# A third row tile in the last steps of attention, five steps a tile, eight sets of row statistics

## The reference

```python
def attn(x):                       # Wq, Wk, Wv, Wo, bo
    q, k, v = heads(x @ Wq), heads(x @ Wk), heads(x @ Wv)
    scores = q @ k.T - slopes * abs(pos_k - pos_q)
    scores = where(pos_k > pos_q, -inf, scores)
    return (softmax(scores / 8) @ v) @ Wo + bo
def ffn(x):                        # w1, b1, w2, b2
    h = round_2^-8(x @ w1 + b1)
    h = round_2^-8(piecewise_linear_gelu(h))       # 33 break points
    return round_2^-8(h @ w2 + b2)
x = x + layernorm(attn(layernorm(x)))
x = x + layernorm(ffn(layernorm(x)))
```

## Time and profile before

| | |
|---|---|
| time, median of 3 runs | 1228.38 us (1227.55 to 1300.74) |
| profiled execution | 1228.59 us |
| span of its slowest core | 1227.1 us (the eight cores: 1222.7 to 1227.1) |
| busy, share of the span | PE 93%, ACT 80%, DVE 61%, POOL 15% |
| 640 to 678 us, of 38 us | ACT busy 38.00, PE 32.80, DVE 18.61 |
| 678 to 711 us, of 33 us | PE busy 29.25, DVE 19.95, ACT 16.86 |

### The profile page before, as it was taken

One profiled execution on the slowest core, in us unless ns is written; L12 is line 12 of the kernel. 1 busy time (PEld: TensorE's weight loads), 2 busy tenths in 40 slices (PEclk: granted clock), 3 DMA queues, 4 the chain that ended last, 5 costly groups with the idle time before them and its releaser, 6 DMA issues.

```text
span 1227.1 us, 26972 instructions; the slowest of 8 cores (1222.7 to 1227.1 us)
## 1 busy us (share of the span) xinstructions
PE 1139.3 (93%) x11162; PEld 640.9 (52%) x11298; DVE 751.6 (61%) x1613; ACT 983.1 (80%) x1217; POOL 180.9 (15%) x357
## 2 busy tenths in 40 slices
PE   2889989999999999999998899879999999999996
PEld 2565556666565666666564444434444444444443
DVE  7876533333434324343344589996888888888843
ACT  3449999999999999999999578887777777777720
POOL 4530010010100100000002243430111111111110
PEclk9999999999999999999999999989999999999999
DMA  9952532343433412111119965656333333333211
GB/s 260 268 158 59 96 72 52 70 83 66 84 57 61 79 34 44 38 23 32 28 36 198 219 219 155 161 118 150 112 112 112 112 112 121 120 122 111 77 69 69
DMA packets 62870, 128.00 MB, mean 104 GB/s; under 512 B 9238, under 2 KB 26134, under 8 KB 62108
## 3 DMA queue, kind: packets, MB, share of 16 engines
q1 hardware_dynamic: 53900, 101.10, 28.2%
q0 software_dynamic: 8848, 25.17, 13.6%
HBM read 117.84 MB, written 25.17 MB: 117 GB/s over the span
## 4 chain that ended last, share of the span: by engine, by line
PE 73%; DVE 13%; ACT 8%; DMA 3%; issue 2%; POOL 1%; SPq 0%; DVEq 0%; POOLq 0%; ACTq 0%
PE pW L948 18%; PE pF L875 14%; PE pjb L316 11%; PE S L409 9%; PE acc L462 9%; PE pjb L348 8%; ACT P L425 6%; DMA xst<-x_full 2%; PE pja L316 1%; DVE x L578 1%; DVE bst L235 1%; DVE bst L236 1%; DVE g L919 1%; DVE kst L326 1%; DVE g L913 1%
## 5 line engine op out<-in xcount | busy, mean ns | idle before, releaser
L425 ACT ACTIVATE P<-S,biasT 128x1024 bf16<-128x1024 f32 (+1 forms) x576 | 563.4, 1078 | 20.9 <-PE S L409 19.1
L875 PE MATMUL pF<-xl2T,w1s 128*128 128x512 bf16 x1002 | 257.7, 384 | 12.3 <-ACT cu L890 11.0
L948 PE MATMUL pW<-w2s,hq 128*128 128x512 bf16 x1003 | 250.8, 380 | 3.3 <-ACT pW L973 2.2
L462 PEld LDWEIGHTS acc<-V,P 128*128 128x128 bf16 x4352 | 162.6, 97 | 53.5 <-DVE ctx L480 11.3
L462 PE MATMUL acc<-V,P 128*128 128x66 bf16 x4352 | 179.1, 193 | 4.1 <-DVE ctx L480 2.4
L409 PE MATMUL S<-Q,K 64*128 64x512 bf16 (+3 forms) x1280 | 173.4, 349 | 8.4 <-ACT P L425 6.6
L875 PEld LDWEIGHTS pF<-xl2T,w1s 128*128 128x128 bf16 x1024 | 100.2, 99 | 132.1 <-ACT cu L890 12.8
L948 PEld LDWEIGHTS pW<-w2s,hq 128*128 128x128 bf16 x1024 | 100.3, 98 | 123.9 <-issue 3.9
L316 PE MATMUL pjb<-xlT,W 128*128 128x512 bf16 x572 | 152.3, 381 | 13.0 <-issue 6.5
L326 DVE CAST kst<-pjb 128x512 bf16<-128x512 f32 x81 | 56.0, 691 | 132.5 <-PE pjb L316 128.7
L890 ACT ACTIVATE cu<-pF,b1s 128x512 int32<-128x512 f32 x128 | 87.7, 685 | 59.2 <-PE pF L875 59.2
(11 more groups left out here) (91 smaller groups left out, 1064.9 us busy)
## 6 DMA issues: line engine op xcount, KB each, us to landing
w1s<-w1bf SPq DMA_DIRECT2D x128, 256.0 KB, 2.7
xst<-x_full SPq DMA_DIRECT2D x32, 512.0 KB, 9.8
K<-kst SPq DMA_DIRECT2D x128, 64.0 KB, 2.0
Q<-kst SPq DMA_DIRECT2D x128, 64.0 KB, 2.3
w1bf<-w POOLq DMA_DIRECT2D x32, 256.0 KB, 4.0
x<-x_full SPq DMA_DIRECT2D x16, 512.0 KB, 5.2
w2s<-w POOLq DMA_DIRECT2D x8, 1024.0 KB, 26.9
x2scr<-x SPq DMA_DIRECT2D x16, 512.0 KB, 4.2
```

Source lines behind the costliest of these rows:

```text
L425: t = put("scalar", lambda io: io.activation(out=P3[:, :, c0:512], in_=S[s][:].rearrange("p (o c) -> p o c", o=2)[:, :, c0:512], func=AF.E ...
L462: io.matmul(acc[:, q * 66:(q + 1) * 66], P[p][:, at:at + 128], zv[:, o, j, hh, :], start=st, stop=sp, skip_group_check=True),
L875: t = put("tensor", lambda io, c=c: io.matmul(pF[b][:], w1s[n % 4][:, c * 128:(c + 1) * 128], xl2T3[g][:, c, :], start=(c == 0), stop=(c = ...
L948: t = put("tensor", lambda io, ft=ft, hf=hf: io.matmul(pO[b][:, hf * 512:(hf + 1) * 512], slot_of(g, ft, tl), w2s[:, ft * 1024 + hf * 512: ...
```

## The change

Three row tiles instead of two go through `c_early` (EARLY = 3). One yield in each half of the projection and the one after the transposes are taken out, so that each copy out of PSUM is listed right behind the matmuls that it waits for, in the same visit: five steps a tile instead of eight, with `c_x2` still in the call after. `ctxTe` and `sume` stay two buffers each and are used in turn. The ring of row statistics has eight slots instead of four. The normalisation of tile 0 and the load for tile 4 come just after `c0(3)`, since `c_parts` starts at n = 3.

```diff
-    NS = 4
+    NS = 8
...
-        EARLY = 2
+        EARLY = 3
...
             C[j, "left"] = t
-            yield
-            t = put("vector", lambda io: io.tensor_copy(out=ctxTe[j][:], in_=pjT[:]),
+            t = put("vector", lambda io: io.tensor_copy(out=ctxTe[j % 2][:], in_=pjT[:]),
                     after=[t, proj_end], inc=True)
             pjs["free"][0] = C[j, "ct"] = t
             yield
...
-                        pj_b[:], ctxTe[j][:, c * 128:(c + 1) * 128],
+                        pj_b[:], ctxTe[j % 2][:, c * 128:(c + 1) * 128],
...
                 t = put("tensor", lambda io, sl=sl: io.matmul(
                     pj_b[:], ones[:], borow[:, sl], start=False, stop=True), after=[t_brow], inc=True)
-                yield
                 pjs["free"][0] = C[j, "a"] = put("vector", lambda io, sl=sl: io.tensor_copy(
-                    out=sume[j][:, sl], in_=pj_b[:]), after=[t, proj_end], inc=True)
+                    out=sume[j % 2][:, sl], in_=pj_b[:]), after=[t, proj_end], inc=True)
                 if hf == 1:
-                    C[j, "sum"] = sume[j]
+                    C[j, "sum"] = sume[j % 2]
                     c_sta(j)
                 yield
             c_x2(j)
...
         c0(EARLY)
+        for j in range(EARLY - 2):
+            c_xl(j)
+            c_load(j + 4)
 
         for n in range(EARLY, 7):
             for _ in c_parts(n):
```

## The result

The changed kernel takes 1236.96 us, median of 3 runs (1236.96 to 1237.2), against 1228.38 before. The ratio is 1.0072 with a 95% interval of 1.0058 to 1.0086: slower by 0.7%, inside the 2% that were counted as no change, but clear of the scatter. One of the three runs of the kernel before took 1300.74 us, with the cores of one die at a lower clock, and the ratio leaves it out. The span of the slowest core is 1235.4 us, 8.3 more than before.

A forecast was written before the change was run, and what follows sets the result against it. Chain taken to run through ACT's exponentials while early tiles are worked on, then DVE's x2 steps; 7.4 + 2.8 - 5.6 + 0 = +4.6 us gives 1233.0 us, forecast range 1229.5 to 1237.5, 8 in 10 from 1226 to 1238.5.

The forecast's parts named there:

- The period taken out of the serial stretch: Between attention's end and `f_mm(0)`: one tile fewer saves one period of DVE's x2 chain, 5.58 us.
- PE has room for the third tile: In attention: a tile's five visits cost PE 9.99 us against ACT's 10.2, so it barely fits; otherwise 0 to 1 us.
- The two waits: At both tile changes in attention: PE waits 4.1 us for `ctxTe`, ACT loses 3.2 and 4.2 us, 7.4 together.
- The low clock: Behind both waits PE drops to half clock, 1.5 us lost each time; 2.8 us taken, bounds 0 to 3.0.
- The transfer: Serial stretch: the x load for tile 4 lands about when x2 wants it; 0 us, up to 2 as bound.
- rival (b): Waits covered or small, but tile 4's x load holds x2 in the serial stretch: 1228 us, -1.5 to +2; chance 0.19.
- From `f_mm(0)` on one to one: From the first feed-forward matmul to the end: same order of work, so the +4.6 us shift carries through unchanged.
- Rival (a): Waits in attention covered, third tile free, serial stretch gives back its period: 1223.3 us without the transfer; chance 0.13.

The follow-up runs named there:

- x2 in two parts: Changed kernel with an early tile's `c_x2` cut in two, x2 itself and its statistics listed in separate visits; ratio 1.0015 to the kernel before.
- The w1 loads behind the x loads: Kernel with x2 in two parts, with SP's four w1 loads listed behind the x loads of tiles 4 and 5; 1223.97 us, ratio 0.9970.
- the statistics behind: The 1223.97 us kernel with an early tile's row statistics also listed behind the next tile's copy to `ctxTe`; 1223.9 us, ratio 0.9969.
- x2 behind the copy: Changed kernel with a tile's `c_x2` listed behind the next tile's copy to `ctxTe` instead of ahead of it; ratio 1.0022 to the kernel before.
- the first experiment: Kernel before with five steps a tile and still two early tiles; ratio 1.0064 to the kernel before, 7.9 us.
- the second experiment: Changed kernel with one yield put back between a tile's transposes and the copy to `ctxTe`, six steps a tile; ratio 1.0054 to the kernel before.

## Why the prediction was right, and where its sizes were off

The direction, the mechanism and the place were right: one DVE queue between two visits, twice, and 1233.0 lay 4.0 us below the measured time. Step by step, for the slowest cores (6 before, 2 in the changed kernel):

- **The period taken out of the serial stretch.** Forecast 5.6 us, measured 31.4 - 26.5 = 4.9. The first x2 step came 703.56 - 693.47 = 10.1 us after the end of attention, not 9.35, as the first Wo matmuls ran at the low clock for longer (15 of them in 5.09 us, where core 6 before took 3.75; cores 0 and 2 before took 5.1 as well). The forecast let DVE's x2 steps set the pace. They still come 5.5 to 5.6 us apart, but the chain of the changed kernel stays on PE, at 4.78 us a tile: the third x2 step ends at 716.03, when PE reaches the matmuls of tile 7. The two are level, so by this estimate a fourth early tile would save PE's 4.8 us and not 5.6; that was not run.
- **PE has room for the third tile.** Right in the main: 40.2 us instead of 39.0 once no long wait is left, where 0 to 1 us was forecast. The forecast took 1.02 us for an exponential, from 33.7 / 33; by the earlier trace rows it is 39.08 / 40 = 0.98, so ten take 9.8 us and PE's 9.99 did not quite fit.
- **The two waits.** Forecast 4.1 us of PE each, measured 4.8 and 4.7. ACT's idle time without the clock was forecast as 3.2 and 4.2 us; the second was measured by itself, 4.20. The first was not. If the low clock adds to its first stop what it adds at the second, 5.67 - 4.20 = 1.47, it would be 5.27 - 1.47 = 3.8, an estimate.
- **The low clock** is the term that was mis-sized most. Forecast 2.8 us for both places, from eight matmuls of the earlier trace rows that lost 1.5 us. Measured 2.3 to 2.7 us at one place alone; with the estimate above it is 13.3 - 4.2 - 3.8 = 5.3 us for both on core 2. The earlier trace rows show only eight matmuls; here half the clock also slowed `av`, the scores and the next piece, all of it on the chain. How long it stays low behind the wait differs: ACT's second stop at the first place is 1.14 us on core 2 and none on core 3.
- **The transfer.** Forecast 0, right for the changed kernel: it waited for no DMA, and moving the load changed nothing. The w2 load was out of the way earlier than forecast (landed at 696.1 on core 2, not near 700). The tie that the prediction named, if the waits cost less, this transfer costs more, is what the kernel with x2 in two parts showed: 1.9 us over the kernel before, inside the -1.5 to +2 of rival (b). The prediction expected the order on SP's queue to matter more than the w2 load beside it; the table under "The w1 loads behind the x loads" shows that both do.
- **From `f_mm(0)` on one to one.** Right within 0.1 us for the slowest cores. On five of the eight, the kernel before was 1.3 to 1.7 us faster there; why is not shown.

Sum for the slowest cores: 13.3 us of ACT's idle time + 1.0 in short stops - 4.9 in the serial stretch = 9.4 us. The slowest core of the changed kernel began its first tile 1.0 us earlier than that of the kernel before, so the spans differ by 8.3 and the medians by 8.6. That 1.0 us has nothing to do with the change; by so much the number came out closer than its terms, which is luck.

Rival (a), the tile for free, needed three things at once that the change didn't have: x2 away from `ctxTe`, away from the accumulator's release, and the x load ahead of w1. With them the kernel takes 1224 us, 0.3% less than before; that is also the best version found, with or without the statistics behind.

## What to carry to other kernels

Steps of background work that are listed in one go on an in-order engine should be looked at for what stands behind them: every operation that the critical engine awaits (here the next operand's copy, the accumulator's release, a mask) is late by the whole string. When steps are merged to save visits, count the longest string between two things that the critical engine needs, not the work in a visit. And when a stretch gets shorter, look again at each transfer that was "just not late" in it.

## What the runs showed of the hardware

Behind each wait of PE of 4.7 to 4.8 us the granted clock was 0.50, and so it was behind one of 3.3 us (x2 behind the copy) and two of 2.5 us (the mask wait of the first experiment, `ctxTe` in the second), on all eight cores each time. Behind one of 1.8 us (`ctx` in the second experiment) it fell on four of the eight. When the second wait was filled with matmuls of no use the clock stayed up, and ACT's idle time there fell from between 6.6 and 6.9 to 4.2 us. A low clock did no harm where PE had time to spare: on core 3 of the kernel before it was 0.50 from 676 to 679 us, with no wait of PE over 1 us ahead of it, no work of an early tile was left for PE there, and the exponentials came without a stop.

An x load of 512 KB on core 6 landed after 18.05 us with four w1 loads of 256 KB ahead of it on its queue and a w2 load beside it on another, and after 9.9 us with only the w2 load beside it. With the w2 load landed it took 4.8 to 6.1 us behind the w1 loads and 3.4 to 4.6 us ahead of them.
